# The feed-forward part of a transformer layer: each of 16 columns computed only for the tokens that chose it

## What is computed

```python
logits = similarity + gate_values                 # one number per token and column, 16 columns
k = max(1, int(C * SPARSITY))                     # int(16 * 0.05) = 0, so k = 1
_, top_idx = jax.lax.top_k(logits, k)
weights = mask * jax.nn.softmax(logits, axis=-1)  # nonzero in the chosen column alone
cols = jax.nn.gelu(jnp.einsum('bsd,cdn->bscn', x, W_cols) + b_cols, approximate=False)
cols = cols * weights[..., None]                  # 16 columns of 64 neurons
y = cols.reshape(Bq, Sq, -1) @ proj_w + proj_b + x
out = layernorm(y) * ln_g + ln_b
```

## Time and profile before

| | us |
|---|---|
| three executions | 2259.39, 2262.02, 2256.68 (median 2259.39) |
| the profiled execution: its time, its span | 2256.26, 2254.5 |
| prologue, up to the first row stage of batch 0 | 230.4 |
| the four groups of one batch in the steady part (1004.58 to 1267.66 us) | 66.9, 61.1, 64.7, 70.5 = 263.1 |
| from the last group that still shared its list with the old ffn to the end (1978 us on) | 276.4 |

### The profile page before, as it was taken

How to read it: one execution, slowest core, us unless ns; L and a number is a source line. 1 busy time by engine, 2 the same in 40 slices (tenths; PEclk the granted TensorE clock), 3 DMA queues, 4 the chain that set the end, 5 groups by cost and what they waited for, 6 DMA issues and landing times. The chain is left out here.

```text
span 2254.5 us, 40933 instructions
## 1 busy us (share of the span) xinstructions
PE 1911.3 (85%) x11110; PEld 1072.1 (48%) x11110; DVE 1599.7 (71%) x5859; ACT 1103.1 (49%) x2142; POOL 632.8 (28%) x848
## 2 busy tenths in 40 slices
PE   5887989888989889889988889898898899986666
PEld 2554455555545455454545555454554554542223
DVE  2325888777878677767887677787777678876673
ACT  2221555545556555445554445565554555543344
POOL 5543333322333333222333213333332233300000
PEclk9887999999999999999999999999999999988778
DMA  8333223334333233344223343332333443223221
GB/s 215 120 75 62 49 46 57 62 67 76 62 62 73 43 57 62 53 86 75 52 44 56 61 76 62 62 75 41 57 62 53 85 76 56 49 41 48 33 33 38
DMA packets 150222, 144.51 MB, mean 64 GB/s; under 512 B 54283, under 2 KB 131483, under 8 KB 143852
## 3 DMA queue, kind: packets, MB, share of 16 engines
q1 hardware_dynamic: 149996, 141.82, 34.4%
HBM read 90.59 MB, written 56.69 MB: 65 GB/s over the span
## 5 line engine op out<-in xcount | busy, mean ns | idle before, releaser
L840 ACT ACTIVATE probs<-scores 128x512 f32<-128x512 f32 (+1 forms) x1280 | 672.4, 555 | 548.4 <-DVE scores L1120 279.0
L1145 DVE CUSTOM_DVE_ANT_0 rows<-rows,near_rows 128x256 f32<-128x256 f32 (+1 forms) x1024 | 416.6, 408 | 184.2 <-PE rows L987 173.5
L954 PE MATMUL scores<-stack_q,stack_k 99*128 99x512 bf16 (+3 forms) x1536 | 440.2, 336 | 66.7 <-ACT probs L840 56.3
L987 PE MATMUL rows<-stack_k,stack_q 96*128 96x256 bf16 (+1 forms) x1024 | 279.5, 279 | 193.8 <-DMA stack_k<-parts_d 123.1
L1120 DVE TENSOR_TENSOR scores<-scores,near_cols 128x256 f32<-128x256 f32 x768 | 329.1, 438 | 88.5 <-PE scores L954 88.2
L1141 DVE TENSOR_REDUCE maxima<-rows 128x1 f32<-128x256 f32 (+1 forms) x768 | 304.1, 396 | 106.9 <-PE rows L991 105.8
L971 PE MATMUL o_bank<-probs,v_aug 128*32 128x512 f32 (+3 forms) x3072 | 321.3, 506 | 3.2 <-ACT probs L840 3.2
L987 PEld LDWEIGHTS rows<-stack_k,stack_q 96*128 96x128 bf16 x1024 | 98.9, 98 | 467.4 <-issue 181.1
L1059 PE MATMUL bank<-w_proj,act_t 128*128 128x256 f32 x1024 | 302.0, 439 | 1.7 <-ACT act_t L899 1.7
L1048 PE MATMUL scores<-xn_t,w_cols 128*128 128x256 f32 x1024 | 287.0, 404 | 2.5 <-ACT others_t L886 2.5
L1150 DVE TENSOR_REDUCE maxima<-rows 128x1 f32<-128x128 f32 (+3 forms) x512 | 248.0, 484 | 48.9 <-PE rows L993 47.1
(11 more groups left out here) (109 smaller groups left out, 2266.8 us busy)
## 6 DMA issues: line engine op xcount, KB each, us to landing
parts_d<-part SPq DMA_DIRECT2D x96, 256.0 KB, 2.7
stack_q<-parts_d SPq DMA_DIRECT2D x192, 128.0 KB, 6.7
stack_k<-parts_d SPq DMA_DIRECT2D x192, 128.0 KB, 7.3
x<-in_x_dram SPq DMA_DIRECT2D x32, 256.0 KB, 3.0
v_d<-v SPq DMA_DIRECT2D x32, 256.0 KB, 2.5
rest_d<-rest SPq DMA_DIRECT2D x32, 256.0 KB, 2.7
v_in<-v_d SPq DMA_DIRECT2D x32, 256.0 KB, 10.7
result<-rest_d SPq DMA_DIRECT2D x32, 256.0 KB, 4.1
```

The costliest lines, as they stand in the source:

```text
L840: act.activation(probs[:, (g * NS + s) % PROBS, h, 0:width], ring[(rings + ring_n[1]) % RING][:, 0:width], ACT.Exp, scale=float(D) ** -0.5 ...
L954: ins = pe.matmul(ring[(rings + ring_n[1]) % RING][:, c0:c0 + w], stack_k[g % 2][:, h, kb * P:(kb + 1) * P], stack_q[g % 2][:, h, q0:q0 + ...
L987: ins = pe.matmul(tile[:, 0:(qb + 1) * P - far], q, keys[:, far:(qb + 1) * P], start=True, stop=True)
L1145: dve.tensor_tensor_reduce(tile[:, 0:w], tile[:, 0:w], near_rows[:, ag * GH + h, 2 * P - w:2 * P], 1.0, LOWEST, ALU.add, ALU.max, maxima[: ...
```

## The change

One column per token means that a batch's tokens can be sorted by column. The new kernel does this on the chip:

- `tally` and `route`, once per batch in group 2 (`ROUTING`): TensorE counts the tokens of each column and each token's place in it with products of 0/1 matrices in bf16; VectorE rounds each column's count up to whole tiles of 64 rows, sums them up (15 small operations with a wait between each two), and has a slot for each token and the column of each of the 32 tiles. Any distribution fits in 1024/64 + 16 = 32 tiles, and always all 32 are computed.
- GpSimd scatters the normalized tokens, with their weights, to their slots in memory (xs_d), by 8 indirect DMAs of 128 rows (`route`), and gathers the results back from ys_d by 8 more (`gather`, beside slot 24 of group 2).
- One step per group, 8 tiles each: `ffn_in` on SyncE's queue, first in the group's list, issues one load of 512 slots and, for each of the 8 tiles, reads the tile's column number from SBUF into a register and issues two loads, of the column's 64 KB of W_cols and 64 KB of proj_w with the bias. `xs_turn` (slots 8 and 10) transposes the tokens; `neurons` (slot 14) is 16 fp32 products of 128x64 by 64, `columns` (slots 18 and 20) 8 of 64x64 by 256; ScalarE applies Gelu and the weight, GpSimd adds xn, and SyncE's queue stores ys.
- `mask_turn`, `skip`, `y2_stats` and the detour over rest_d go. `finish_begun` and `finish` (statistics, normalization, gain, sum) move from one chunk in every group to two chunks in group 3 and two in group 0, beside slots 2 to 16; x is fetched a second time (`again`) instead of rest_d. At the end of the kernel the last two chunks are finished after the last scores.
- The weights of the ffn stand in memory in a new layout (w1_d, w2_d), copied there at the start, no longer in SBUF.
- The prologue holds no ffn but one step at its end; CLOSING and OPENING hold no TensorE work of the ffn. Gelu now stands in one slot of a group (14), before in two places.

```diff
-EM = E * N // P
+SLOT = 64
+SLOTS_B = (T // SLOT + E) * SLOT
+FFN_STEPS = NC
+HALVES = SLOTS_B // SLOT // FFN_STEPS
+PAIRS = HALVES // 2
+ROW = C + 2
+ROUND = float(1 << 23)
...
-OPENING = [("stats", None), ("columns", 0), ("columns", 1), ("columns", 2)]
-CLOSING = [("load", None), ("neurons", (0, 0)), ("neurons", (0, 1)), ("pv", NS - 1), ("o_out", 1),
-           ("neurons", (1, 0)), ("neurons", (1, 1)), ("neurons", (2, 0)), ("shift", None),
-           ("neurons", (2, 1)), ("neurons", (3, 0)), ("neurons", (3, 1)), ("o_turn", 1), ("shift_turn", None)]
+BESIDE = {2: [('widen', None), ('finish_begun', 0)],
+          4: [('center', None)],
+          6: [('x_turn', None)],
+          7: [('finish', 0)],
+          8: [('xs_turn', 0)],
+          9: [('qk_begun', 0), ('qk', 0)],
+          10: [('xs_turn', 1)],
+          12: [('v', 0), ('finish_begun', 1)],
+          14: [('neurons', None), ('hidden', None)],
+          15: [('qk_begun', 1)],
+          16: [('qk', 1), ('finish', 1)],
+          18: [('columns', 0)],
           19: [('v', 1)],
+          20: [('columns', 1)],
           21: [('gate', None), ('o_turn', 0)],
           23: [('qk_turn', 0), ('choose', None)],
+          24: [('gather', None)],
           25: [('left', 0), ('tie', None), ('middle', 0)],
           26: [('choice', None), ('y_turn', 0)],
+          27: [('weigh', None)],
           28: [('project_begun', 0)],
           29: [('project', 0)],
+          30: [('qk_turn', 1), ('tally', None)],
+          31: [('left', 1)],
+          32: [('y_turn', 1), ('route', None)],
           34: [('middle', 1)],
           35: [('project_begun', 1)],
           37: [('project', 1)]}
+OPENING = [("ffn_in", None), ("again", 0), ("stats", None)]
+
+ALONE = [("stats", None), ("center", None), ("x_turn", None), ("qk_begun", 0), ("qk", 0), ("qk_begun", 1), ("qk", 1),
+         ("hidden", None), ("v", 0), ("gate", None), ("v", 1), ("choose", None), ("qk_turn", 0), ("left", 0),
+         ("tie", None), ("choice", None), ("weigh", None), ("middle", 0), ("qk_turn", 1), ("left", 1), ("tally", None),
+         ("route", None), ("middle", 1)]
+FFN_ALONE = [("ffn_in", None), ("xs_turn", 0), ("xs_turn", 1), ("neurons", None), ("columns", 0), ("columns", 1)]
+CLOSING = [("load", None), ("pv", NS - 1), ("o_out", 1), ("shift", None), ("o_turn", 1), ("shift_turn", None)]
...
+                    elif stage == "ffn_in":
+
+                        yb, k, step = step_of(b, g)
+                        if g < 0:
+                            sp.wait_ge(columns_in, LATE_LOADS * 16)
+                        if k == 0:
+                            sp.wait_ge(columns_routed, yb + 1)
+                            alone(sp)
+                            sp.wait_ge(scattered[0], (yb + 1) * (CT * 16))
+                            alone(sp)
+                            sp.wait_ge(scattered[1], (yb + 1) * ((NT - CT) * 16))
+                            alone(sp)
+                        wait(sp, ys_out, step * 16)
+                        alone(sp)
+                        sp.dma_start(xs[:, :, :], xs_d[k * HALVES * SLOT:(k + 1) * HALVES * SLOT, :]
+                                     .rearrange("(q p) f -> p q f", p=P)).then_inc(ffn_loaded, 16)
+                        for half in range(HALVES):
+                            at = k * HALVES + half
+                            col = sp.value_load(column_i[at:at + 1, 0:1], min_val=0, max_val=E - 1)
+                            sp.dma_start(w1[:, half, :, :], w1_d[col]).then_inc(ffn_loaded, 16)
+                            lane = (half % 2) * N
+                            sp.dma_start(w2[lane:lane + N, half // 2, :], w2_d[col]).then_inc(ffn_loaded, 16)
...
+                    elif stage == "route":
+
+                        pool.wait_ge(slots_ready, fb + 1)
+                        alone(pool)
+                        wait(pool, ffn_loaded, fb * (FFN_STEPS * FFN_LOADS * 16))
+                        alone(pool)
+                        if g < 0:
+                            pool.wait_ge(columns_in, LATE_LOADS * 16)
+                        for j in range(NT):
+                            pool.indirect_dma_start(xs_d[:, :], bass.IndirectOffsetOnAxis(slot_i[:, j:j + 1], 0),
+                                                    xn_all[:, j, :], None).then_inc(scattered[j >= CT], 16)
...
+                    elif stage == "gather":
+
+                        wait(pool, gathered, b * (NT * 16))
+                        alone(pool)
+                        pool.tensor_copy(slot_kept[:, :], slot_i[:, :]).then_inc(slots_kept, 1)
+                        pool.wait_ge(slots_kept, b + 1)
+                        alone(pool)
+                        pool.wait_ge(ys_out, (b + 1) * (FFN_STEPS * 16))
+                        alone(pool)
+                        wait(pool, finished, b * NC)
+                        alone(pool)
+                        for j in range(NT):
+                            pool.indirect_dma_start(gathered_y[:, j, :], None, ys_d[:, :],
+                                                    bass.IndirectOffsetOnAxis(slot_kept[:, j:j + 1], 0)) \
+                                .then_inc(gathered, 16)
...
+                    elif stage == "tally":
+
                         pe.wait_ge(chosen, n * CHOSEN_STEPS + 7)
-                        for t in range(CT):
-                            ins = pe.transpose(bank[0:E, t * P:(t + 1) * P], others[:, t, :], ident[:, :])
+                        for j in range(NT):
+                            ins = pe.matmul(bank[:, 0:E], ones_b[:, :], chosen_one[:, j, :],
+                                            start=(j == 0), stop=(j == NT - 1))
+                        ins.then_inc(bank_filled[i], 1)
+                    elif stage == "route":
+
+                        pe.matmul(bank[:, 0:NT * E], sooner[:, :], chosen_one[:, :, :].rearrange("p j e -> p (j e)"),
+                                  start=True, stop=False)
...
+                        pe.wait_ge(ring_drained, tile_n + 1)
+                        tile = ring[(rings + ring_n[1]) % RING]
+                        for pair in range(PAIRS):
+                            for h in range(2):
+                                for k in range(KC):
+                                    ins = pe.matmul(tile[h * N:(h + 1) * N, pair * SLOT:(pair + 1) * SLOT],
+                                                    w1[:, pair * 2 + h, k, :],
+                                                    xs_t[:, pair, k, h * SLOT:(h + 1) * SLOT],
+                                                    start=(k == 0), stop=(k == KC - 1))
+                        ins.then_inc(ring_filled, 1)
...
+                        pe.wait_ge(ring_drained, ring_n[0] + (needs + (1 + RING)))
+                        alone(pe)
+                        for q in range(2):
+                            for h in range(2):
+                                lanes = slice(h * N, (h + 1) * N)
+                                ins = pe.matmul(bank[lanes, q * C:(q + 1) * C], act_t[lanes, 2 * arg + q, :],
+                                                w2[lanes, 2 * arg + q, 0:C], start=True, stop=True)
+                        ins.then_inc(bank_filled[i], 1)
...
+                        step(3)
+                        last = E // 2
+                        dve.tensor_scalar(ends[0][:, last:], caps[:, 2, :], float(SLOT), None, ALU.mult) \
+                            .then_inc(route_step, 1)
+                        for d in range(4):
+                            step(4 + d)
+                            src, dst = ends[d % 2], ends[1 - d % 2]
+                            dve.tensor_tensor(dst[:, last:], src[:, last:], src[:, last - (1 << d):last + E - (1 << d)],
+                                              ALU.add).then_inc(route_step, 1)
...
```

451 lines of the change are left out of this document (250 added, 201 removed).

## The result

The changed kernel takes 2649.87 us (median of 4 runs, 2644.09 to 2654.46) against 2260.14 for the kernel before: 1.1725 times as long, 95% interval 1.1692 to 1.1758. The forecast was 2334, with a range up to 2480. The sign was right, the size was not: +390 instead of +78.

A forecast was written before the change was run, and what follows sets the result against it. The prediction took VectorE to bound the score parts, TensorE the openings and the stack load the stretches behind the last score. 2256 + 94 (+14.1 per batch times 6.7) - 36 + 20 = 2334 us, range 2130 to 2480.

The forecast's parts named there:

- Columns out of OPENING: Group openings: without the columns pieces they get shorter, -10.7 us per batch, bounds -8 to -11.
- Clock: Group start and score part: longer TensorE idle time lowers the granted clock, costing +2 us per batch, bounds 0 to +6.
- Rows: Score parts: 22 more row stages per batch at 0.53 us each on VectorE, +12.8 us, bounds 0 and 18.
- VectorE's own ffn work: VectorE: column scaling goes (3.2 us), 15 small operations come (3.3 us), finishing only shifts between groups; 0 per batch.
- TensorE in the score part: Score parts: TensorE gets slightly more work, but VectorE bounds; 0 per batch, with +5 left in the range.
- Boundary and tables: Group boundaries and ScalarE: rest_d fetch goes (-3), Gelu table changes once per group instead of twice (-2); -5 us per batch.
- Indirect DMAs: GpSimd, group 2: sixteen at 1.2 us each delay VectorE and the next stack load, +10 us per batch, bounds 0 and +25.
- Fetch on SyncE's queue: Token and weight loads, reads at 0.7 us: 1.2 us of waiting per group, +5 us per batch, bounds 0 and +30.
- Prologue: Before the first group: four chunks lose their ffn and save up to 15 us each; -36 us, bounds 15 and 60.
- A: Score parts: VectorE's idle tenth takes the moved work in, descriptors are cheap, fetch always early; about 2118 us, chance 0.27.
- B: SyncE's queue becomes the bound: a register read costs 1.5 us, weights come late in 31 groups; about 2500 us, chance 0.10.
- C: GpSimd: descriptors are written slowly, 2.5 us per indirect DMA, so +10 becomes +25; 2434 us, chance 0.06.

The follow-up runs named there:

- e9: Kernel before with both fp32 products of neurons and 12 of 16 columns products left out per group, so the ffn is not computed: 2264 us against 2254.
- e8: Changed kernel with 8 extra unread 128x256 fp32 products in the opening of each group: 2638 us against 2643 without.
- e4: Changed kernel with scatter and gather (the indirect DMAs) moved behind `middle` 1 of group 2 on GpSimd's queue: 2591 us.
- e19: Changed kernel with its loop over batches 1 to 5 written out, nothing else: 2600 us.
- e3: Changed kernel without the eight register reads per step, each tile taking a fixed column's weights, so the layer is not computed: 2554 us.
- e17: Changed kernel with fetch, xs_turn, neurons and columns placed as before, gather in group 3, finishing in slots 20 to 27, scatter behind `middle` 1: 2509 us.
- e14: Changed kernel with `again` first, indirect DMAs behind `middle` 1, 8 extra products per opening, and the prologue's second stack load ahead of the fetch: 2577 us.
- e5: Changed kernel with 16 extra unread 128x256 fp32 products per group as its last stage, behind `shift_turn`: 2679 us.
- e7: Changed kernel with three of four fetches issued in the group before, `again` ahead of the fetch, and indirect DMAs behind `middle` 1 of group 2: 2680 us.
- e18: e17 with row stages from slot 6, shift loads on ScalarE's queue, and finishing in slots 1 to 8 and 22 to 31: 2533.45 us.

## Why the prediction was wrong, point by point

*Neurons out of CLOSING, 0: right.* Stretches 76.1 us against 76.7, and 73.5 in e9, from which the products were taken.

*Columns out of OPENING, -10.7: right as a reading, wrong as a gain.* The openings fell by 10.1. But the pieces had a second use: behind them the clock was up for the score part, and without them up to 14 to 16 us came back there.

*Clock, +2 with bounds 0 to 6: the first step that failed.* I took it from the late group of the earlier trace rows, 38.4 us at 0.81, and concluded that the clock costs little where TensorE doesn't bound. That group has no front. With it TensorE and VectorE are both full, and a first third at half clock is late work for both. e8 and e9 measure up to +14 and +16. Three more steps failed with it, each worked out below: VectorE's ffn work and TensorE's in the score part, both put at 0 by balancing busy times, and the start of the fetch. A batch came to +53.0 instead of +14.1; of these 39 us the clock is about 13, VectorE 13, TensorE 12 and the fetch 8, while rows and indirect DMAs, costed too high, give 8 back.

*Rows, +12.8: right in kind.* At 0.32 us each, 22 rows are +7.

*VectorE's own ffn work, 0: too low.* Group 2 is still 8.0 us longer than group 1 in e4, with both groups of indirect DMAs out of the way (0.2 before): `tally` and `route`. In the changed kernel their operations wait for one another, 2.7 us in a row at 1372.78 to 1375.5, and a bias addition of a score stands behind them. That all 8 us are theirs is argued from this; no run takes them out. Groups 0 and 3 lie 6.7 and 5.9 above group 1 in e19, without the jump, against 3.8 and 3.6: +5 for the finishing of two chunks.

*TensorE in the score part, 0: too low.* Between e3 and e17, neither with a wait for the fetch in group 1, that group is 3.6 us shorter with no ffn in slots 8 to 20. Of this 0.6 goes to two row stages less in e17, perhaps more, since VectorE is busy 36.5 us there and 38.3 in e3; the granted clock of that part is 0.92 and 0.91, so the clock is not it. About +3 a group, +12 a batch; the 64-wide products stand exactly where the front fills TensorE. This is a difference of two kernels with several edits between them, so it is the least certain entry.

*Boundary and tables, -5: about right.* The stretch behind group 3 lost 3.8 of its 22.3 us.

*Indirect DMAs, +10: right.* 1.25 us from start to start, 4.0 us of VectorE's wait on GpSimd, the load behind group 2 9.3 instead of 4.7 us after the last score: 7.5 per batch by e4.

*Fetch on SyncE's queue, +5 with bounds 0 to 30: too low.* The read was right (0.66), and so was the wait where no jump stands, 0.3 to 2.8 us a group against the 1.2 that I took. The start of the fetch was not: behind the four jumps of the loop it comes 9 us late. Together 12 to 14 in a batch with a jump. I had put the longer boundary of four groups before to the fetch of rest_d; a jump stands there as well, and behind group 3 of batch 5, which has that fetch and no jump, the stretch from the first load is 16.5 us like the others. So the jump was in the rows, misread.

Sum of the measured pieces of the score parts: clock 15, rows 7, fetch 13, indirect DMAs 4, `tally` and `route` 8, finishing 5, TensorE's ffn 12: 64 of 63.6. That they close is partly luck: e14 shows that they overlap.

*Prologue, -36: wrong sign.* The first stack load went out 13.7 us earlier (144.52), and then two waits that I hadn't costed:

```profile
220.05 1.94 PE L1155 MATMUL bank<-ident,xs 128*128 128x128 f32 x8 [23.28 <-DMA w<-w_d]
...
250.04 0.50 PE L1093 MATMUL rows<-stack_k,stack_q 96*128 96x128 bf16 x2 [18.30 <-DMA stack_k<-parts_d]
```

The first step's fetch has nothing to hide behind. And the second stack load stood on SyncE's queue behind the store of that step's result (issued at 233.17, the load at 233.83), so behind the whole step, though the fetch was out by 218. With the load ahead of the fetch the first group starts at 224 to 234 us instead of 250; in e17, where the load stays behind the fetch but `columns` and their store are out of the prologue, it goes out at 207.14 and the group starts at 222. *From 1978 us on, +20:* measured +26.4.

*Rivals.* A is dead: the score part took nothing in. B had the right place and the wrong price: a read is 0.66 us, and taking the reads out gave 84 us of the 390, not 166. C is dead: 0.94 to 1.25 us per indirect DMA, 0.96 for most.

## What to carry to other kernels

Ask of work that seems to fill a wait or an opening what it does for those behind it: before it is moved, take its instructions out and leave everything else; here that one run (e9) would have shown that the TensorE work to be saved was worth nothing. Work that cost no time in a gap did cost time where its replacement landed: here the score parts took 64 us more per batch although TensorE and VectorE are busy for 64% and 61% of the span, and waited for each other, as all of them walk one list in order. And when something is added to a queue, cost what stands behind it, not only who waits for it.

## What the runs showed of the hardware

- The clock at a group's start went with TensorE's own work there: with 7 us of filler until 2.6 us ahead of the start, then 0.94 us of work in 5 us, it fell from 1.00 to 0.50 (e5); with 8 products inside the opening it was 1.00 from the first score on (e8).
- A jump back of a loop held SyncE's queue for 9 us, each of four times, with the stack load's transfers under way and nine instruction packets instead of one; written out, the loop had 2.0 us there (e19).
- An indirect DMA of 128 rows takes GpSimd 0.96 us for most, 1.25 at most, and 1.25 from start to start; a read of a register from SBUF costs SyncE's queue 0.66 us.
- With sixteen indirect DMAs beside a full load, and the fetch early, VectorE and ScalarE stood for 16 and 18 us without a semaphore (e7); the cause is not settled.
- A 24 KB transfer from another engine's queue reached its reader 9.2 us after the issue beside a running load (e18).
